# The high halves of the ropes and of the probabilities: made by VectorE instead of ScalarE

## The reference, cut to what matters

```python
h = einsum('bct,bcd->bdt', x, cond_weights[itok])        # conditioned input, 64 tokens x 1024
q, k, v = (h @ ((qw - 8) * repeat(scales, 128)) for each) # 4-bit weights; 32 q heads, 8 k/v heads of 128
q, k = rope(q), rope(k)                                   # x * cos + rotate_half(x) * sin
scores = einsum('bhqd,bhkd->bhqk', q, k) / sqrt(128)      # causal mask
ctx = einsum('bhqk,bhkd->bhqd', softmax(scores), v)
x = x + (ctx @ dequantized(qw_o))
x = x + ffn(cond2(x))                                     # routed LoRA feed-forward, not touched
```

## Time and profile before

| | us |
|---|---|
| median of 3 runs | 2125.24 (2123.53 to 2125.55) |
| the profiled execution | 2124.41 |
| its span, from first to last instruction | 2122.6 |
| attention loop (from the first step to the last output tiles) | from about 119 to about 1780 |

### The profile page before, as it was taken

The page is one execution under the profiler, slowest core; times in us unless marked ns, Lnnn a source line. Parts: engine busy times, 40 slices in busy tenths (PEclk is TensorE's granted clock), DMA queues, the critical chain, the costliest instruction groups (busy, mean ns, idle before and its releaser), DMA issues.

```text
span 2122.6 us, 40823 instructions
## 1 busy us (share of the span) xinstructions
PE 1887.3 (89%) x15074; PEld 1027.1 (48%) x15074; DVE 1467.6 (69%) x2211; ACT 1187.5 (56%) x1949; POOL 244.8 (12%) x206
## 2 busy tenths in 40 slices
PE   3679999998999899999999999999999846779999
PEld 3334555554555455545554455455554423555444
DVE  6477678776877686768777877777778755995222
ACT  2566666675667566656666666566665512980000
POOL 0011111111111111111111111111111000230000
PEclk8899999999999999999999999999999988999999
DMA  6211112020202020202020101111110211110111
GB/s 199 73 40 31 45 37 71 2 61 22 71 6 69 9 71 10 72 12 61 16 65 24 50 26 56 42 32 36 46 50 21 60 30 41 36 42 36 49 40 50
DMA packets 100601, 96.07 MB, mean 45 GB/s; under 512 B 13340, under 2 KB 75172, under 8 KB 100388
## 3 DMA queue, kind: packets, MB, share of 16 engines
q1 hardware_dynamic: 99748, 93.09, 14.8%
q10 hardware_dynamic: 640, 0.13, 0.0%
HBM read 84.81 MB, written 8.39 MB: 44 GB/s over the span
## 4 chain that ended last, share of the span: by engine, by line
PE 69%; DVE 11%; issue 11%; ACT 4%; SPq 3%; DMA 1%; POOL 0%; DVEq 0%; ACTq 0%; POOLq 0%
PE sa L1294 13%; PE sbk L1294 11%; PE pj L1226 9%; PE pj L1228 8%; PE tp L1238 8%; PE cx L1412 4%; PE cx L1275 2%; PE ex L1226 2%; PE ex L1412 2%; PE sa L1412 2%; PE ex L1228 2%; PE tp L1252 2%; ACT pj L1040 1%; DVE kb L677 1%; PE tp L1264 1%
## 5 line engine op out<-in xcount | busy, mean ns | idle before, releaser
L1040 ACT ACTIVATE pj<-pj,ratio 128x512 f32<-128x512 f32 x896 | 588.0, 661 | 373.4 <-PE pj L1228 370.0
L1226 PE MATMUL pj<-hid,wts 128*128 128x512 f16 x1024 | 393.3, 384 | 43.0 <-ACT pj L1040 26.8
L1228 PE MATMUL pj<-hid,wts 128*128 128x512 f16 x1024 | 392.5, 383 | 0.0
L479 POOL TENSOR_TENSOR work<-work 128x512 f32<-128x512 f32 x160 | 203.0, 1269 | 1444.7 <-DVE work L671 1444.7
L1294 PE MATMUL sa<-wts,cb 128*128 128x512 f16 x768 | 212.5, 381 | 24.9 <-DVE y L736 24.9
L1040 ACT ACTIVATE ex<-ex,ratio 128x512 f32<-128x512 f32 x224 | 148.0, 661 | 134.7 <-PE ex L1228 134.0
L1294 PE MATMUL sbk<-wts 128*128 128x512 f16 x768 | 218.6, 384 | 2.2 <-DVE y L736 2.2
L1294 PE MATMUL sbk<-wts,cb 128*128 128x512 f16 x768 | 216.7, 381 | 1.8 <-DVE y L736 1.8
L1294 PE MATMUL sa<-wts 128*128 128x512 f16 x768 | 210.6, 379 | 0.0
L1238 PEld LDWEIGHTS tp<-wts,hid 128*128 128x128 f16 x3072 | 182.2, 98 | 30.2
L1238 PE MATMUL tp<-wts,hid 128*128 128x128 f16 x3072 | 192.5, 220 | 0.0
(11 more groups left out here) (193 smaller groups left out, 2738.9 us busy)
## 6 DMA issues: line engine op xcount, KB each, us to landing
work<-qo_d SPq DMA_DIRECT2D x64, 256.0 KB, 3.3
work<-so_d SPq DMA_DIRECT2D x64, 256.0 KB, 4.2
wts<-qq_d SPq DMA_DIRECT2D x35, 256.0 KB, 2.9
y<-x_d SPq DMA_DIRECT2D x4, 2048.0 KB, 7.9
work<-wb_d SPq DMA_DIRECT2D x32, 256.0 KB, 2.8
out_d<-y SPq DMA_DIRECT2D x16, 512.0 KB, 2.7
int_even<-qq_d SPq DMA_DIRECT2D x29, 256.0 KB, 3.1
work<-qv_d SPq DMA_DIRECT2D x16, 256.0 KB, 7.1
```

The source lines that it names most:

```text
L479: gp.tensor_tensor(ra[:, u % 2, :], ra[:, u % 2, :], rb[:, :], ALU.add).then_inc(S["rope_sum"], 1)
L1040: act.activation(unit_bank[u][:, :], unit_bank[u][:, :], ACT.Copy, scale=ratio[:, KT * u + j:KT * u + j + 1]).then_inc(S["u_scaled"], 1)
L1226: mm(bank[:, :], w_int[:, u, j, :], hid[:, 0, j, CH * c:CH * (c + 1)], start=j == 0, stop=False, skip_group_check=True)
L1228: mm(bank[:, :], w_int[:, u, j, :], hid[:, 1, j, CH * c:CH * (c + 1)], start=False, stop=True, skip_group_check=True).then_inc(S["u_done"], 1)
```

## The change

The two kinds of high half move from ScalarE's list into VectorE's. VectorE gets `rope_high` and `prob_high`, each a `tensor_copy` from f32 to f16 with the waits that ScalarE had, directly in front of its own `rope_split` or `prob_split`. ScalarE loses `rope_hi` and `prob_hi`. The semaphores `rope_hi` and `probs_hi` stay, and the splits still wait for them. The values computed are the same. The high half of the values (`v_hi`) and of the context (`ctx_hi`) stay on ScalarE.

```diff
+            def rope_high(p4, u):
+                dve.wait_ge(S["rope_sum"], upto(p4, NU, u + 1))
+                need(dve, "scores_done", upto(p4, 2, 0))
+                dve.tensor_copy(rope_write(u, 0), rope_sum_of(u)).then_inc(S["rope_hi"], 1)
+
...
+            def prob_high(p4, h):
+                dve.wait_ge(S["probs"], upto(p4, 2, h + 1))
+                need(dve, "tp_done", upto(p4, 2, h))
+                dve.tensor_copy(pp[:, 0, :], sm[:, h, :, :].rearrange("p b s -> p (b s)")).then_inc(S["probs_hi"], 1)
+
...
                 soft_mask(p4, 0)
+                rope_high(p4, 4)
                 rope_split(p4, 4)
...
                 soft_shift(p4, 1)
+                prob_high(p4, 0)
                 prob_split(p4, 0)
...
                 pt_copy(p4, 0)
+                prob_high(p4, 1)
                 prob_split(p4, 1)
...
                 pt_copy(p4, 1)
                 if ahead:
+                    rope_high(ahead, 0)
                     rope_split(ahead, 0)
                 ctx_lo(p4, 0)
...
                 if ahead:
+                    rope_high(ahead, 1)
                     rope_split(ahead, 1)
                     rope_mul(ahead, 2)
...
                 if ahead:
+                    rope_high(ahead, 2)
                     rope_split(ahead, 2)
...
                 if ahead:
+                    rope_high(ahead, 3)
                     rope_split(ahead, 3)
...
                 rope_mul((0, 0), u)
+                rope_high((0, 0), u)
                 rope_split((0, 0), u)
...
-            def rope_hi(p4, u):
-                a = ra[:, u % 2, :].rearrange("p (b s) -> p b s", b=CB)
-                dst = kb[:, 0, :].rearrange("p (b s) -> p b s", b=CB) if u == 0 else qb[:, (u - 1) // 2, 0, :, (u - 1) % 2, :]
-                act.wait_ge(S["rope_sum"], upto(p4, NU, u + 1))
-                need(act, "scores_done", upto(p4, 2, 0))
-                act.activation(dst, a, ACT.Copy).then_inc(S["rope_hi"], 1)
...
-            def prob_hi(p4, h):
-                act.wait_ge(S["probs"], upto(p4, 2, h + 1))
-                need(act, "tp_done", upto(p4, 2, h))
-                act.activation(pp[:, 0, :], sm[:, h, :, :].rearrange("p b s -> p (b s)"), ACT.Copy).then_inc(S["probs_hi"], 1)
...
-                    elif r == 2:
-                        rope_hi(p4, 4)
...
-                    elif r == 6:
-                        prob_hi(p4, 0)
...
-                    elif r == 9:
-                        prob_hi(p4, 1)
...
-                        if r in HI_AT:
-                            rope_hi(ahead, HI_AT.index(r))
...
-            HI_AT = (11, 14, 18, 22)
...
-                if r in HI_AT:
-                    rope_hi((0, 0), HI_AT.index(r))
```

## The result

| | before | after |
|---|---|---|
| median (lowest to highest), us | 2125.39 (2123.53 to 2127.27) | 2169.98 (2162.69 to 2171.80) |
| profiled execution, us (its span) | 2124.41 (2122.6) | 2162.69 (2160.9) |
| mean granted clock of TensorE in it | 0.975 | 0.964 |

The change makes the kernel slower: ratio 1.0203, 95% interval 1.0178 to 1.0229. The forecast was 2139.4 in a range of 2125.5 to 2146. The sign is right, but the loss is three times the one forecast, and the time lies outside the range.

What follows compares the result with a forecast made beforehand. The prediction took TensorE, with small holes, to bound the kernel; 12.8 + 4.05 - 2.6 + 1.9 - 2.0 = +14.2 us on the median 2125.24 gave 2139.4, range 2125.5 to 2146.

Steps and rivals of the forecast that it cites:

- What bounds the kernel, and where the change acts: TensorE, busy 89% of the span, bounds the kernel; the change acts only through holes, 2 to 5 us a step.
- Price of the copies: On VectorE 0.42 us a copy, 0.45 in a chain, longer when held by GpSimd's rope sum.
- Terms 1 and 2: K copy held before `ctx_lo`: +0.44 in 29 steps, +12.8; its removal from ScalarE shrinks round 12's hole, net 0.
- Rivals A and B: K copy not held by GpSimd's sum: A at 0.42 us, 2126, chance 0.17; B at 0.68 us, 2133, chance 0.08.
- C: Rival: copy takes 0.68 us and is held by GpSimd's sum; +25, 2150, chance 0.04.
- Terms 3 and 4: Rope 4 before `soft_max(0)`, c = 1 and step 29: +4.05; probabilities 0, c = 2 round 7: -2.6.
- Terms 5, 6 and 7: Probabilities 1, ropes 1 to 3: 0; step 30 and tail: +1.9; prologue and step 0: -2.0.
- Rival D: Faster: ScalarE was the bound at round 12, so its hole's delay is gained; -10, 2115, chance 0.06.
- the sum: All terms added to +14.2 us, each hole's delay priced as listed idle time plus some 0.16.

Runs made afterwards that it cites:

- K behind `ctx_lo`: K's high half and split put behind `ctx_lo` in the changed kernel: 2095.97, ratio 0.9864; the split alone likewise in the kernel before: 2099.37, ratio 0.9883.
- K's copy alone: Kernel before with one move alone, the K rope's high half made by VectorE instead of ScalarE: 2156.31, ratio 1.0149.
- dummy operations: Kernel before, nothing moved, dummy VectorE maximum added between K split and `ctx_lo`: one 2136.09, ratio 1.0053; two 2154.74, ratio 1.0147.

## Why the prediction was wrong, step by step

- *What bounds the kernel, and where the change acts:* right for the holes. They add up as forecast; the rest of the difference is lower clock, three quarters of it behind one of them.
- *Price of the copies:* right. 0.415 forecast as 0.42; held by GpSimd's sum it takes 0.975. The Trainium skill (SBUF — State Buffer, "Who interferes with whom") was cited for a copy that shuts out, or is shut out by, a whole GpSimd instruction; the trace agrees: 0.99 us beside the sum, 0.42 behind it (K behind `ctx_lo`).
- *Terms 1 and 2, K's chain and the hole of round 12:* right, +12.8 forecast, +26.0 - 12.6 = +13.4 measured. Rivals A and B fall with the row of 0.99, C with the row of 415 ns.
- *Terms 3 and 4:* right, +4.05 and -2.6 forecast, +3.7 and -2.7 measured; the extra 0.45 of step 29, which term 3 counts, stands in front of the first `weigh_values` (1.94 to 2.37). In step 5 the copy stands in front of the row maximum, and ScalarE's exp starts behind it; TensorE then idles 0.89 where it idled 0.43:

```profile
375.74 0.41 DVE L678 CAST qb<-work 128x512 f16<-128x512 f32 x1
...
379.31 0.63 ACT L1069 ACTIVATE work<-work 128x512 f32<-128x512 f32 x1 [2.67 <-DVE work L704]
...
380.54 0.39 PE L1221 MATMUL pj<-hid,wts 128*128 128x512 f16 x1 [0.89 <-ACT pj L1058]
```

- *Terms 5, 6 and 7:* right within a microsecond or two. In the other steps the wait of the first `weigh_values` didn't grow. Step 1 starts 2.6 earlier, for 2.0. The tail moved as a block: SP's issues stand 38.8 us later than in the earlier trace rows, and the hole behind them, listed as 24.89 there, is 24.31.

```profile
1741.45 47.23 SPq L422 DMA_DIRECT2D work<-wse_d  x32
...
1802.45 1.89 PE L1289 MATMUL sa<-wts,cb 128*128 128x512 f16 x4 [24.31 <-DVE y L746]
```

- *Rival D, ScalarE as the bound at round 12:* it falls as it was put, but half of it held: the hole of round 12 did close, and its 12.6 us were paid back at once in front of `weigh_values`. With that wait out of the way they are a gain.
- *The step that failed:* the sum. It took the delay of a hole as "its listed idle time plus some 0.16", that is, it priced a longer wait at its own length. That holds for the waits of 1.44 and 1.77 us. For those of 2.3 it leaves out what comes after: 11 of 22 were followed by some 8 matmuls at half speed. No term of the sum and no rival has it. The missing term is the lower clock, +22.4 us in the profiled execution where the chain gave 13.4: 16.4 behind that wait, 1.0 behind the wait of step 29, and 5.0 at the starts of steps, which the change isn't shown to cause. The median is another 7 above that execution.

The trace of before had rows for it, which the prediction didn't look for: it read the waits but not the matmuls behind them. At the starts of steps 12 and 8, where the loop over the groups turns, TensorE is delayed by 2.92 and 3.21 us; behind the first the next matmuls are 0.43 apart, behind the second they are not. TensorE of the kernel before, step 12, then step 8:

```profile
724.33 0.61 PE L1226 MATMUL pj<-hid,wts 128*128 128x512 f16 x1 [2.76 <-DVE work L671]
724.73 0.64 PE L1228 MATMUL pj<-hid,wts 128*128 128x512 f16 x1
725.16 2.44 PE L1294 MATMUL sbk<-wts 128*128 128x512 f16 x6
...
520.28 0.39 PE L1226 MATMUL pj<-hid,wts 128*128 128x512 f16 x1 [3.05 <-DVE work L671]
520.51 0.38 PE L1228 MATMUL pj<-hid,wts 128*128 128x512 f16 x1
520.72 1.46 PE L1294 MATMUL sbk<-wts 128*128 128x512 f16 x6
```

Such a fall stands behind two of the five waits at these places, and behind none of the 22 of 1.4. The forecast's own wait of 2.3 lies between, so these rows couldn't say whether the clock would fall, but they would have given a case of its own: at 1.7 us a step, two fifths to all of 22 steps make 15 to 37 us on top of 2139, or 2154 to 2177, where the measured median lies. This is said in hindsight. Instead the range ended at 2146, with only errors in the copies' price above it.

What stays open: why a wait of the same length lowers the clock in one step and not in another (steps 5 and 9 of the changed kernel), why some executions have more such steps than others, and with them why the changed kernel loses 14 us more than K's copy alone; and why all five long waits at the starts of steps lowered it in the profiled execution of the changed kernel, where two did before.

## What to carry to other kernels

A wait of TensorE is not always paid for with its length alone: before adding to one, look in the trace at the matmuls behind the longest waits that are already there, and give the fall of the clock a term and a rival of its own. The order of a vector engine's list counted for more than which engine makes a copy: the same seven moves were worth +45 us, -3, or -16, depending on what stood in front of the one instruction for which TensorE waited. And a gain upstream of a wait that is set elsewhere is given back there, as round 12's was here, so remove the wait first and measure the move then.

## What the runs showed of the hardware

TensorE's granted clock fell to its lower level (1.2 GHz, 0.43 us for 512 columns) after waits that stood in an otherwise full stretch: behind none of 22 waits of 1.4 us (kernel before), none of 22 of 1.7 to 1.8 and 4 of 22 of 2.0 to 2.1 (dummy operations), and 11 and 13 of 22 of 2.3 (changed kernel, K alone); behind none of the 7 waits of 1.6 to 1.7 in c = 3 of the changed kernel. In the eleven traces together it fell behind all 5 waits of 2.37 to 2.39 in front of the first `weigh_values` of step 29 and none of the 6 of 1.94, and at 41 of 55 starts of steps with waits of 2.9 to 3.6. So a longer wait made a fall likelier, but length alone didn't decide it. It came back after some 8 matmuls. The fall showed in the spacing of matmuls and in the clock column of a short stretch (0.63), while the mean over the whole execution moved by 0.011 only.
